# One product of 512 columns that nobody reads, behind every pair of chunks of the score stage

## The reference

```
h = einsum('ni,hio->nho', x, W)            # x normalised, 8 heads of 32
hs, hd = h[src], h[dst];  diff = hd - hs
lin = hs·a1 + hd·a2 + diff·a3 + |diff|·a4 + (hs*hd)·a5     # per edge and head
alpha = where(lin > 0, lin, 0.2 * lin)
...
e = exp(alpha - segment_max(alpha)[src]);  att = e / (segment_sum(e)[src] + 1e-16)
out = segment_sum(att * hd, src)
```

## Time and profile before

| | before |
|---|---|
| median of 3 runs | 2841.8 us (2838.65 to 2847.17) |
| the profiled execution | 2848.16 us, its span 2846.4 us |
| TensorE busy | 2225.9 us, 78% |
| VectorE, ScalarE, GpSimd busy | 1644.8, 1458.0, 1402.0 us |
| mean granted TensorE clock | 0.809 |
| the score stage, from its first matmul to its last differences | 1537.3 to 2158.4 us |

### The profile page before, as it was taken

One profiled execution on the slowest core, in us unless ns is written; L12 is line 12 of the kernel. 1 busy time (PEld: TensorE's weight loads), 2 busy tenths in 40 slices (PEclk: granted clock), 3 DMA queues, 4 the chain that ended last, 5 costly groups with the idle time before them and its releaser, 6 DMA issues. The chain is left out here.

```text
span 2846.4 us, 62154 instructions
## 1 busy us (share of the span) xinstructions
PE 2225.9 (78%) x14844; PEld 1813.8 (64%) x14845; DVE 1644.8 (58%) x4125; ACT 1458.0 (51%) x3570; POOL 1402.0 (49%) x1434
## 2 busy tenths in 40 slices
PE   4888866677777589999936899888885899759990
PEld 3655533444444479999925788878775677549980
DVE  8888853333333643333266667777678788853337
ACT  6778843333333334333446556656564888433334
POOL 0000047777777123333225666676671999425540
PEclk9999976655656689999966766777786999979995
DMA  3310025533333511111125767777772888642223
GB/s 108 108 39 20 18 92 178 179 105 105 104 105 103 132 46 37 35 35 37 43 104 162 217 203 208 215 220 208 213 220 49 273 268 265 222 153 70 70 65 139
DMA packets 182438, 367.94 MB, mean 129 GB/s; under 512 B 30426, under 2 KB 67716, under 8 KB 182126
## 3 DMA queue, kind: packets, MB, share of 16 engines
q1 hardware_dynamic: 118489, 208.65, 21.6%
q0 software_dynamic: 53760, 148.67, 19.9%
q10 hardware_dynamic: 10133, 9.97, 1.0%
HBM read 275.35 MB, written 91.83 MB: 129 GB/s over the span
## 5 line engine op out<-in xcount | busy, mean ns | idle before, releaser
L950 PE MATMUL sum_ps<-weightsL_w 128*128 128x256 f32 x880 | 389.9, 593 | 179.1 <-DMA weightsL_w<-y_gnn,sum_index 108.3
L883 POOL DMA_INDIRECT scores_rows<-h_gnn,scores_index x440 | 427.2, 971 | 190.9 <-issue 119.4
L883 POOL DMA_INDIRECT weightsL_w<-y_gnn,sum_index x440 | 416.8, 947 | 132.7 <-issue 128.7
L950 PEld LDWEIGHTS sum_ps<-weightsL_w 128*128 128x128 f32 x880 | 231.2, 289 | 337.6 <-issue 303.8
L965 DVE TENSOR_TENSOR sums_acc<-sums_acc,sum_ps 128x256 f32 x440 | 185.3, 421 | 372.2 <-PE sum_ps L950 326.8
L2059 PE MATMUL scores_diff_ps<-scores_minus,scores_node 128*128 128x128 bf16 x2640 | 368.5, 262 | 0.0
L1568 ACT ACTIVATE sums_acc<-expertsL_hid_ps,expertsL_b 128x128 f32<-128x128 f32 x704 | 197.6, 372 | 301.3 <-PE expertsL_hid_ps L1517 301.0
L1517 PE MATMUL expertsL_hid_ps<-sums_acc,expertsL_w 128*128 128x128 f32 x2816 | 335.7, 276 | 3.9 <-DVE sums_acc L1588 2.8
L2059 PEld LDWEIGHTS scores_diff_ps<-scores_minus,scores_node 128*128 128x128 bf16 x2640 | 318.4, 135 | 30.9
L2057 PE MATMUL scores_diff_ps<-all_ident,scores_rows 128*128 128x128 f32 x880 | 334.0, 380 | 3.7 <-DVE scores_node L2160 2.0
L1517 PEld LDWEIGHTS expertsL_hid_ps<-sums_acc,expertsL_w 128*128 128x128 f32 x2816 | 325.6, 193 | 4.4 <-issue 4.3
(11 more groups left out here) (432 smaller groups left out, 4128.2 us busy)
## 6 DMA issues: line engine op xcount, KB each, us to landing
saved_gnn<-scores_rows SPq DMA_DIRECT2D x220, 264.0 KB
sum_rows<-saved_gnn SPq DMA_DIRECT2D x220, 264.0 KB, 3.1
weightsL_w<-in_L_ffn_W SPq DMA_DIRECT2D x16, 1024.0 KB, 8.7
weightsL_w<-in_L_ffn_w SPq DMA_DIRECT2D x32, 512.0 KB, 9.3
scores_lanes<-slot_lanes SPq DMA_DIRECT2D x44, 320.0 KB
sort_low_b<-low_lanes SPq DMA_DIRECT2D x32, 416.0 KB, 3.5
weightsL_w<-ys_L SPq DMA_DIRECT2D x6, 1280.0 KB, 12.7
weightsL_w<-y_gnn,sum_index POOLq DMA_INDIRECT x440, 2.7
```

The lines of the kernel that those rows point to most:

```text
L883: pool.indirect_dma_start(out=self.rows[s] if isinstance(self.rows, list) else self.rows[:, s, :], out_offset=None, in_=table[:, :], in_of ...
L950: last = nc.tensor.matmul(ps[s % banks][:, 0:D], pick[h][:, s % HALF, :], g.rows[s], start=True, stop=True)
```

## The change

One PSUM bank more is reserved (`idle_ps`, the eighth of eight), and TensorE's `reduce` gets one call of `idle_products` at its end, behind the instruction that increments `reduced`. It waits for nothing, and nobody waits for it.

```diff
+        idle_ps = m.ps("idle_ps")
         with nc.Block() as block:
...
                 def reduce(i, p):
...
                         last = nc.tensor.matmul(out, joint[:, p % HP, j, :], c["by_head"][:, :], start=False, stop=True)
                     last.then_inc(reduced, 1)
+                    idle_products(nc, c, idle_ps, 1)
```

## The result

The changed kernel takes 2812.97 us (median of six runs, 2811.49 to 2818.75), beside 2845.59 us for the kernel before (six runs, 2838.65 to 2849.18): a ratio of 0.9889, 95% interval 0.9867 to 0.9912. The medians are 32.6 us apart, the profiled executions (2813.41 and 2848.16 us) 34.8 us. The forecast was 49 us less, 2793 us, with a range to 2830.

A forecast was written before the change was run, and what follows sets the result against it. The score stage was taken as bound by TensorE at the low clock, VectorE at the high, GpSimd second. 1.14 us a half, times 43, is 49 us: 2841.8 - 49 = 2793 us, range 2768 to 2830.

The forecast's parts named there:

- What bounds the stage: Score stage: TensorE sets low-clock halves (16.5 to 16.8 us), VectorE high-clock ones (12.2 us); GpSimd is the second limit.
- The clock, rising: Score stage: with the product, TensorE's clock rises after the shortest low stretch seen, some 3.5 us.
- The clock, falling: Score stage: TensorE's wait at the second pair still makes the clock fall once in nearly every half.
- The gap: TensorE's wait at a half's second pair, behind VectorE's tile-number load: 2.6 to 3.0 us becoming 1.5 to 1.9.
- the prediction's own line: Score stage: half time drawn straight from 12.2 us (always high clock) to 16.65 us (always low).
- The product's cost: TensorE, score stage: each added product takes 0.215 us at the high clock level, 0.42 at the low.
- A half: Score stage, five pairs: from 14.24 to 13.1 us, between the line's 13.4 and GpSimd's 12.7; 49 us in all.
- What would show it: Score-stage signs: PEclk about 0.87, low stretches 3 to 4 us, L2071's 72.2 us wait for `join` shrinking to 30 to 50.
- The clock doesn't follow: Rival, score stage: the product doesn't help the level rise, only costs; 2890 us (2850 to 2930); chance 0.1.
- GpSimd at its limit everywhere: Rival, score stage: clock high nearly always, a half takes 12.7 us, 66 us less, 2776 us; chance 0.2.
- Gain and cost even out: Rival, score stage: low stretches two or three times the shortest, halves of 14.1 us, 2836 us; chance 0.1.

The follow-up runs named there:

- two products: The changed kernel with two 512-column products a pair instead of one: 2796.81 us, ratio 0.9855 to the kernel before.
- twelve narrow products: The changed kernel with twelve bf16 products of 24 columns replacing the 512-column one: ratios 1.0181, 1.0171, 1.0133 to the kernel before.

## Why the prediction was right, and what was off

**What bounds the stage** held. Low halves are TensorE's, high ones VectorE's, and GpSimd's slack shrank from 67.5 to 23.6 us as forecast (about 20).

**The clock, rising** was the step that carried the sum, and it held in kind: no low stretch is longer than 6.8 us where the longest was 34.1. The size was off. I took the shortest stretch seen, 3.5 us, for all; 8 of the 20 are of that length, 12 twice as long, and the mean is 5.5. With two products it is 3.4.

**The clock, falling** was mis-sized. "One fall in nearly every half still" should have been one in every second half, 20 in 44: the long tile load stands in the first half of a turn only. The earlier trace rows showed one such load, and I took it for all of them. The reasons given for the falls were weak too. The gap was to shrink by up to 1.1 us; in the first halves it went from 3.0 to 2.7 us at the median. And the bracket from 1.06 us (level kept) to 2.6 us (level lost) was drawn from three waits, while 9 of the 27 falls of the same trace came behind waits of 1.0 to 1.7 us.

**Luck.** The two errors, stretches too short and falls too many, work against each other: 44 x 3.5 = 154 us at low were forecast and about 113 measured. With stretches of the measured 5.5 us in every half, the prediction's own line would give 13.9 us a half and 2829 us, an estimate at the very end of the range.

**The product's cost** was over-estimated, 0.14 us at high for 0.215 and 0.36 at low for 0.42.

**A half** at 13.1 us came out at 13.22 (14.3 and 12.1 by turns), so the term "1.14 us a half, times 43, is 49 us" measured 1.02 x 42 = 43 us. The stage as a whole, to its last sum, went from 624.9 to 586.2 us, 38.7 less. The stretch ahead of the first L2155 took 7.2 us both times, but the one behind the last took 23.8 us where it was 19.7. There TensorE waits for gathered rows, once in the kernel before and three times in the changed one:

```profile
PE scores_diff_ps L2057 <- DMA scores_rows<-h_gnn,scores_index: 1.5, 1, 1.5
...
PE scores_diff_ps L2058 <- DMA scores_rows<-h_gnn,scores_index: 3.8, 3, 2.1
```

The other stages of the two executions add 4 us (2.2 ahead of the stage, 1.8 behind it), which I can't tell from their scatter; 34.8 us are left, 32.6 between the medians.

**What would show it**: PEclk 0.87 was forecast, 0.90 came. The wait of L2071 was to shrink to 30 to 50 us and grew to 83.9: it is the wrong sign to look for, because a TensorE at the high level waits more, not less, while the gap stays.

**The rivals.** "The clock doesn't follow" is out by the windows above; twelve narrow products are nearly what it described, products that cost and don't raise the level, and they lose 1.3 to 1.8%. "GpSimd at its limit everywhere" was not reached: even two products leave a half of 13.02 us. It shows at the end of the stage, in the waits for gathered rows above. "Gain and cost even out" rested on long low stretches with one product, which don't occur.

The Trainium skill ("TensorE: Matmul & The Clock Gate", "Loop structure matters more than you think") has it that matmuls stay warm when they follow each other without a long wait. By that rule only cost would have been left for the product. The runs contradict it for this mixture: 16.04 busy us of 16.70 at 0.50 before, and the twelve narrow products.

## What to carry to other kernels

When TensorE is busy and its clock still low, look at what it streams and not at how busy it is: with narrow products and a weight load for each the level rose late, and one wide product per group of them brought it back within 6.8 us here, for 0.14 us at the high level. Before that, look at where the engine waits before the level falls: in the changed kernel one wait of some 2.7 us in each turn of 26 us cost nearly every turn a low stretch, and its origin was a register load on another engine. Shortening that load at its source brought about as much (2805.32 against 2839.79 us), though mostly through VectorE's own time and little through the clock. Whether the two gains add up, no run here shows: they were put together only on chips of the slower kind.

## What was not expected of the hardware

- The load of ten numbers into VectorE's registers takes a median of 2.7 us (2.3 to 3.6) from an address that is no multiple of 16 bytes from the table's start, and a median of 0.85 to 1.08 us from one that is; twelve numbers from an aligned address were as fast as ten. Only the address and the count were changed in the first halves.
- The level of the clock is no matter of busy time alone: on one chip it stayed at 0.50 with TensorE busy for 96.32 of 105.60 us (twelve narrow products), and rose behind a stretch with 7.78 of 13.60 (one wide product).
- Two kinds of chip: the kernel before takes 2839.79 us on one chip of the experiments and 3179.82 to 3214.57 us on three others. DMA shares were lower there, not higher (0.51 to 0.55 in this stage), and TensorE waits without a visible releaser, 111.2 us in this stage. The cause stays open.
